# Splitting the last head's value product of an attention kernel into halves of two row tiles, with the turned weights' high half stored by key tile

## What is computed

```python
def _cross_attention(q_in, kv_in, wq, bq, wk, bk, wv, bv, wo, bo, bias_k, bias_v):
    ...
    logits = jnp.einsum('bqhk,bthk->bhqt', qh, kh) / scale
    weights = jax.nn.softmax(logits, axis=-1)
    ctx = jnp.einsum('bhqt,bthk->bqhk', weights, vh).reshape(b, q_len, H * K)
    return ctx @ wo + bo
...
    x = res + _cross_attention(h, xf_2, wq2, bq2, wk2, bk2, wv2, bv2, wo2, bo2, bias_k2, bias_v2)
    h = _layer_norm(x, ln_mlp_scale, ln_mlp_offset)
    h = jax.nn.gelu(h @ w_fc1 + b_fc1, approximate=False) @ w_fc2 + b_fc2
    return x + h
```

## Time and profile before

| | us |
|---|---|
| median of three runs (2645.69 to 2649.01) | 2648.83 |
| the profiled execution | 2647.3 |
| its span, from the first to the last instruction | 2645.5 |
| TensorE busy in it | 2588.6 |
| VectorE, ScalarE, GpSimd busy | 1724.0, 1506.7, 1321.5 |

### The profile page before, as it was taken

The page is one execution under the profiler, slowest core; times in us unless marked ns, Lnnn a source line. Parts: engine busy times, 40 slices in busy tenths (PEclk is TensorE's granted clock), DMA queues, the critical chain, the costliest instruction groups (busy, mean ns, idle before and its releaser), DMA issues.

```text
span 2645.5 us, 48709 instructions
## 1 busy us (share of the span) xinstructions
PE 2588.6 (98%) x17432; PEld 2144.1 (81%) x17432; DVE 1724.0 (65%) x2630; ACT 1506.7 (57%) x2350; POOL 1321.5 (50%) x750
## 2 busy tenths in 40 slices
PE   7999999999999999998999999999999999999989
PEld 6777788888888888886877777888888888888867
DVE  6999765656656656664279996665665665666641
ACT  4999555545445555544459994555545455555543
POOL 1244246666544666554613433466656456655634
PEclk9999999999999999999999999999999999999999
DMA  7312025345423445451462110344535134544411
GB/s 199 100 50 68 33 68 128 97 121 131 102 69 87 109 109 130 110 124 57 151 144 90 54 63 33 93 103 117 134 98 130 41 98 105 131 113 119 119 64 64
DMA packets 88386, 261.80 MB, mean 99 GB/s; under 512 B 20113, under 2 KB 33697, under 8 KB 81841
## 3 DMA queue, kind: packets, MB, share of 16 engines
q1 hardware_dynamic: 88240, 259.80, 36.9%
HBM read 135.45 MB, written 6.83 MB: 54 GB/s over the span
## 4 chain that ended last, share of the span: by engine, by line
PE 92%; DVE 3%; ACT 2%; issue 1%; DMA 1%; SPq 1%; POOL 1%; DVEq 0%; ACTq 0%; POOLq 0%
PE ps_m L1016 21%; PE ps_t L1016 19%; PE ps_s L1016 16%; PE ps_m L1260 7%; PE ps_t L1260 6%; PE ps_t L1140 6%; PE ps_m L1155 5%; PE ps_s L1124 4%; PE ps_m L1140 3%; PE ps_m L1193 1%; PE ps_m L1026 1%; POOL pT L503 1%; ACT pT L690 0%; ACT p L816 0%; DMA stg_qk<-in_w0q 0%
## 5 line engine op out<-in xcount | busy, mean ns | idle before, releaser
L503 POOL TENSOR_TENSOR pT<-pT,pT 128x1024 fp32r<-128x1024 f32 x224 | 540.1, 2411 | 505.3 <-ACT pT L690 500.7
L690 ACT ACTIVATE pT<-pT 128x1024 fp32r<-128x1024 f32 x224 | 237.9, 1062 | 319.6 <-DMA pT<-pb 319.6
L816 ACT ACTIVATE p<-ps_s,nm 128x1024 f32<-128x1024 f32 x256 | 284.8, 1113 | 201.0 <-DVE nm L1668 200.4
L1665 DVE TENSOR_REDUCE nmx<-ps_s 128x1 f32<-128x1024 f32 x256 | 309.8, 1210 | 119.9 <-PE ps_s L1016 119.8
L1016 PE MATMUL ps_s<-kT,qT 128*128 128x512 f32 x1536 | 384.2, 392 | 3.0 <-DVE qT L1650 3.0
L1684 DVE STREAM_TRANSPOSE pb<-p 128x1024 f32<-128x1024 f32 x224 | 278.1, 1241 | 104.7 <-ACT p L816 100.6
L1016 PEld LDWEIGHTS ps_s<-kT,qT 128*128 128x128 f32 x1536 | 281.5, 188 | 60.0 <-DVE qT L1650 4.7
L1592 DVE CUSTOM_DVE_ANT_0 sm<-ps_s,mask 128x1024 f32<-128x1024 f32 x256 | 309.7, 1210 | 5.7 <-PE ps_s L1124 3.0
L772 ACT ACTIVATE p<-sm,nm 128x1024 f32<-128x1024 f32 x256 | 293.7, 1147 | 33.1 <-DVE nm L1592 29.4
L1016 PE MATMUL ps_t<-ctxT,wa 128*128 128x512 f32 x1080 | 256.7, 391 | 0.0
L1016 PE MATMUL ps_m<-hT,wa 128*128 128x512 f32 x1008 | 243.1, 392 | 3.6 <-ACT g L978 3.6
(11 more groups left out here) (144 smaller groups left out, 4462.1 us busy)
## 6 DMA issues: line engine op xcount, KB each, us to landing
pT<-pb SPq DMA_DIRECT2D x896, 128.0 KB, 2.3
stg_qk<-in_wqk SPq DMA_DIRECT2D x40, 1024.0 KB, 7.5
stg_vo<-in_wo SPq DMA_DIRECT2D x48, 512.0 KB, 3.5
wob<-in_wo SPq DMA_DIRECT2D x32, 512.0 KB, 3.6
stg_vo<-in_wv SPq DMA_DIRECT2D x32, 512.0 KB, 3.6
q_stack<-scr_q SPq DMA_DIRECT2D x48, 128.0 KB, 4.0
st_ctx<-in_ctxT SPq DMA_DIRECT2D x8, 512.0 KB, 5.8
bv_row<-scr_bv SPq DMA_DIRECT2D x32, 128.0 KB, 5.7
```

What stands on the lines that cost most here:

```text
L503: return nc.gpsimd.tensor_tensor(out, x, f32(hi), ALU.subtract)
L690: return nc.scalar.activation(out, in_, ACT.Copy)
L816: nc.scalar.activation(p[t % 2][:], ps_s[t % 2][:], ACT.Exp, bias=nm[:, i:i + 1], scale=SCALE1, accum_out=sums[:, i:i + 1]).then_inc(exp_d ...
L1665: nc.vector.tensor_reduce(nmx[:, i:i + 1], ps_s[t % 2][:], AX.X, ALU.max, negate=True)\
```

## The change

The high half `pT[0]` is stored by key tile, `[P, ST, 4, P]`, so that what one matmul streams lies in one piece; the low half keeps its layout, because the DMAs write it. The value product now leaves its columns in the stored order, and `hi_c` and `lo_c` put them into the order of the rows when they read PSUM. In the tail before the MLP the last head's product is done in two halves of two row tiles (`values_half`, 256 columns), the first of them ahead of tile 3's turn. Each half goes by half-size copies into `qT[0]`, which is no longer needed there, and its two outputs follow it. Outputs 2 and 3 of the first head move between these steps. VectorE's statistics and aggregates of rows 0 and 1 are taken between the halves, and those of rows 2 and 3 after them, so `norm` has no aggregate left to make. After the root ScalarE runs a Gelu of one element per partition into a new tile `ahead`, whose result nobody reads.

```diff
--- before.py
+++ after.py
@@ -62,8 +62,8 @@
...
 L_K0, L_PV1, L_OUT1, L_K1, L_V, M_LAST = (15, 17), 16, (18, 19, 20, 21), (22, 23), (24, 25), 26
-E_V2, E_V3, E_PV0, E_T0, E_T1, E_OUT0, E_T2, E_T3 = 0, 1, 2, 3, 5, (7, 8, 9, 14), 10, 12
-E_PV1, E_OUT1, M_END = 15, (16, 17, 18, 19), 20
+E_V2, E_V3, E_PV0, E_T0, E_T1, E_OUT0, E_T2, E_T3 = 0, 1, 2, 3, 5, (7, 8, 14, 18), 9, 12
+E_PV1, E_OUT1, M_END = (11, 17), (15, 16, 19, 20), 21
 M_S = [M_START0, M_START0 + M_START - 2 + PAIRS * M_PAIR - M_PAIR + M_LAST]
@@ -122,6 +122,7 @@
...
         cols0q = sb("cols0q", [P, 4], F32)
+        ahead = sb("ahead", [P, 1], F32)
         ones = sb("ones", [P, P], F32)
@@ -181,7 +182,7 @@
...
         turned_at = at[0]
-        pT = sb("pT", [P, 4, ST * P], F32R, 2)
+        pT = [sb("pT_hi", [P, ST, 4, P], F32R), sb("pT_lo", [P, 4, ST * P], F32R)]
         pb = sb("pb", [P, 4, ST * P], F32)
@@ -248,7 +249,7 @@
...
         moved_hi, moved_lo = sem("moved_hi"), sem("moved_lo")
-        px_done, c_hi = sem("px_done"), sem("c_hi")
+        px_done, c_hi, c_half = sem("px_done"), sem("c_hi"), sem("c_half")
         bv_made, bv_out = sem("bv_made"), sem("bv_out")
@@ -305,7 +306,30 @@
...
-            return x[:].rearrange("p j (s t n) -> p s j t n", s=ST, t=LT)[:, 4 * q:4 * q + 4, :, lt, :]
+            if x == 0:
+                return pT[0][:].rearrange("p s j (t n) -> p s j t n", t=LT)[:, 4 * q:4 * q + 4, :, lt, :]
+            return pT[1][:].rearrange("p j (s t n) -> p s j t n", s=ST, t=LT)[:, 4 * q:4 * q + 4, :, lt, :]
+        def high_block(j):
+            return pT[0][:, :, j, :]
+        def low_block(j):
+            return pT[1][:, j, :].rearrange("p (s n) -> p s n", s=ST)
+        def in_rows(x):
+            return x.rearrange("p (j t n) -> p t j n", j=4, t=LT)
+        def of_rows(x):
+            return x[:].rearrange("p (t j n) -> p t j n", t=LT, j=4)
+        def half_in_rows(x):
+            return x[:, 0:256].rearrange("p (j t n) -> p t j n", j=4, t=2)
+        def half_of_rows(x, i):
+            return x[:, i * 256:(i + 1) * 256].rearrange("p (t j n) -> p t j n", t=2, j=4)
@@ -591,7 +615,7 @@
...
                             pool.wait_ge(moved_hi, 4 * x + j + 1)
-                            lo(pT[1][:, j, :], f32(pT[1][:, j, :]), pT[0][:, j, :]).then_inc(moved_lo, 1)
+                            lo(low_block(j), f32(low_block(j)), high_block(j)).then_inc(moved_lo, 1)
@@ -825,12 +849,12 @@
...
                             act.wait_ge(m_filled, rt + n + q + 1)
-                            copy(turned_in(pT[0], q, t % LT), turned_from(bank1(n + q))).then_inc(t_hi, 1)
+                            copy(turned_in(0, q, t % LT), turned_from(bank1(n + q))).then_inc(t_hi, 1)
...
                             act.wait_ge(moved_in[j], 64 * (x + 1) + 16)
-                            copy(pT[0][:, j, :], f32(pT[1][:, j, :])).then_inc(moved_hi, 1)
+                            copy(high_block(j), f32(low_block(j))).then_inc(moved_hi, 1)
@@ -840,7 +864,11 @@
...
                         act.wait_ge(m_filled, rt + n + 1)
-                        copy(cT[0][:], bank1(n)[:]).then_inc(c_hi, 1)
+                        copy(of_rows(cT[0]), in_rows(bank1(n)[:])).then_inc(c_hi, 1)
+                    def hi_c_half(n, i):
+                        act.wait_ge(m_filled, rt + n + 1)
+                        copy(half_of_rows(qT[0][0], i), half_in_rows(bank1(n))).then_inc(c_half, 1)
@@ -960,14 +988,19 @@
...
                     turned(n + (L_T2 if more else E_T2), 6)
+                    if not more:
+                        hi_c_half(n + E_PV1[0], 0)
                     turned(n + (L_T3 if more else E_T3), 7)
...
                         hi_column(n + L_K0[0], 1, 0, k_half(0, 0))
-                    hi_c(n + (L_PV1 if more else E_PV1))
-                    if more:
+                        hi_c(n + L_PV1)
                         hi_column(n + L_K0[1], 1, 0, k_half(0, 1))
+                    else:
+                        hi_c_half(n + E_PV1[1], 1)
+                        act.sem_inc(c_hi, 1)
                 root(b * ROWS + 3)
+                nc.scalar.activation(ahead[:], cols0q[:, 0:1], ACT.Gelu)
                 turn_hi(b * 3 + 2)
@@ -1249,7 +1282,7 @@
...
                         free1(n)
-                        out = bank1(n)[:].rearrange("p (t j n) -> p t j n", t=LT, j=4)
+                        moving = (lambda st: pT[0][:, st, :, :], lambda st: pT[1][:, :, st * P:(st + 1) * P])
                         for st in range(ST):
@@ -1257,18 +1290,29 @@
...
                             for i, (a, c) in enumerate(PASSES):
-                                mm = nc.tensor.matmul(out, v[a][:, st, h * P:(h + 1) * P],
-                                                      pT[c][:, :, st * P:(st + 1) * P]
-                                                      .rearrange("p j (t n) -> p t j n", t=LT),
+                                mm = nc.tensor.matmul(bank1(n)[:].rearrange("p (j n) -> p j n", j=4),
+                                                      v[a][:, st, h * P:(h + 1) * P], moving[c](st),
                                                       start=st == 0 and i == 0, stop=st == ST - 1 and i == 2)
...
-                    def output(ns, h, of, lts):
+                    def values_half(n, i):
+                        free1(n)
+                        for st in range(ST):
+                            moving = (pT[0][:, st, :, i * 64:(i + 1) * 64],
+                                      pT[1][:, :, st * P + i * 64:st * P + (i + 1) * 64])
+                            for k, (a, c) in enumerate(PASSES):
+                                mm = nc.tensor.matmul(bank1(n)[:, 0:256].rearrange("p (j n) -> p j n", j=4),
+                                                      v[a][:, st, P:2 * P], moving[c],
+                                                      start=st == 0 and k == 0, stop=st == ST - 1 and k == 2)
+                        mm.then_inc(m_filled, 1)
+                    def output(ns, h, of, lts, results=cT):
...
                             free1(n)
-                            passes(bank1(n)[:], lambda x, c: cT[x][:, lt * P:(lt + 1) * P],
+                            passes(bank1(n)[:], lambda x, c: results[x][:, lt * P:(lt + 1) * P],
                                    lambda q, c: wo[q][:, h, :], 1).then_inc(m_filled, 1)
@@ -1376,25 +1420,32 @@
...
                     pe.wait_ge(vo_lo, b * VO_B + 2 * f + 3)
-                    lts = LT if more else LT - 1
-                    output(out0[:lts], 0, n + (L_PV0 if more else E_PV0), range(lts))
-                    turned(n + (L_T2 if more else E_T2), 6)
-                    turned(n + (L_T3 if more else E_T3), 7)
                     if more:
+                        output(out0, 0, n + L_PV0, range(LT))
+                        turned(n + L_T2, 6)
+                        turned(n + L_T3, 7)
                         pe.wait_ge(qk_lo, 2 * (b * QK_B + 2 + f) + 4)
                         project_k(n + L_K0[0], 0, 0)
-                    else:
-                        output(out0[lts:], 0, n + E_PV0, range(lts, LT))
-                    freed(n + (L_T3 if more else E_T3) + 1)
-                    values(n + (L_PV1 if more else E_PV1), 1)
-                    if more:
+                        freed(n + L_T3 + 1)
+                        values(n + L_PV1, 1)
                         project_k(n + L_K0[1], 0, 1)
-                    output(out1, 1, n + (L_PV1 if more else E_PV1), range(LT))
-                    if more:
+                        output(out1, 1, n + L_PV1, range(LT))
                         for i in range(2):
...
                         project_v(n + L_V[0], 0)
+                    else:
+                        output(out0[0:2], 0, n + E_PV0, range(2))
+                        turned(n + E_T2, 6)
+                        freed(n + E_T1 + 1)
+                        values_half(n + E_PV1[0], 0)
+                        turned(n + E_T3, 7)
+                        for i in range(2):
+                            output(out0[2 + i:3 + i], 0, n + E_PV0, range(2 + i, 3 + i))
+                            output(out1[2 * i:2 * i + 2], 1, n + E_PV1[i], range(2 * i, 2 * i + 2), qT[0])
+                            if i == 0:
+                                freed(n + E_T3 + 1)
+                                values_half(n + E_PV1[1], 1)
@@ -1495,11 +1546,12 @@
...
-            def norm(k, eps):
-                for lt in range(LT):
+            def norm(k, eps, lts=range(LT)):
+                for lt in lts:
                     mm = nc.vector.bn_aggr(mean_var[:, lt, :], stats[:, lt, :])
-                link(mm)
+                if len(lts) > 0:
+                    link(mm)
                 nc.vector.tensor_scalar(lnv[:, 0, :], mean_var[:, :, 1], eps, 0.25, ALU.add, ALU.mult).then_inc(var_done, 1)
@@ -1671,8 +1723,8 @@
...
                             dve.wait_ge(t_hi, h0 + k + 2 * (t % LT) + q + 1)
```

(56 more changed lines are left out.)

## The result

The changed kernel takes 2630.69 us (median of four runs, 2628.61 to 2632.62), the kernel before 2648.06 beside it (2645.69 to 2649.01). The ratio is 0.9938, with a 95% interval of 0.9925 to 0.9950: 17.4 us less by the medians, 16.4 by the ratio. 2631 us had been forecast. The profiled execution took 2630.09 us, against 2647.3.

The account below looks back on a forecast made before the run. TensorE, busy 98% of the span, was taken to bound the loops, with hand-overs deciding outside them. Gains of 8.7 + 7.2 + 2.1 = 18.0 us from 2647.3 gave 2629.3, plus 1.5 for the median: 2631 us, range 2622 to 2641.

Parts of the forecast that it names:

- Part 1: Value products in the loops: high half stored by key tile, 5.46 us each instead of 5.60, gaining 8.7 us in all.
- rival (b): In the loops, GpSimd's subtraction slows on reading 8 runs and TensorE waits before first-head products: about 2684 us, 5%.
- TensorE has no idle time around them, so it all counts: In the loops, the whole 8.7 us saved on value products was claimed to shorten the kernel.
- the 0.3 named as a sign: In the loops, each turn 0.3 us shorter was to show that the value products had become faster.
- Rival (a): Value product: run count isn't what slows it, so the new layout gains nothing; 2639.5 us, 15%.
- Part 2: Tail, last head's product in halves: variance step 3.6 us sooner per batch, 7.2 us in all.
- the walk: Batch 0's tail followed hand-over by hand-over: halves start at 1210.8 and 1216.7, variance step at 1225.05 instead of 1228.70 us.
- The added wait: Tail: tile 3's copies queue behind the first half's, ready 1.9 us later, costing TensorE only 0.4 us.
- Rival (c): Tail: the halves bring nothing because copies queue on ScalarE and VectorE; 7.2 us lost, 2638 us, 6%.
- Part 3: MLP: one-element Gelu after the root loads the table ahead, saving 1.05 us per batch, 2.1 us in all.
- The clock at the turn: Before the MLP: first 16 hidden-projection matmuls take 6.11 or 3.91 us by clock, 2.2 us either way, outside the total.
- The sum: Whole kernel: 8.7 + 7.2 + 2.1 = 18.0 us saved, profiled execution 2629.3 us, median rounded to 2631.

Follow-up runs that it names:

- the two kernels with the early copy: Changed kernel with ScalarE's copy of the query weights' high half moved ahead of row tile 6's exponential, without and with 16 spare-bank matmuls before the turn: 2626.6 and 2620.42 us.
- early_filled: Changed kernel with ScalarE's query-weight high-half copy ahead of row tile 6's exponential, plus 16 matmuls into a spare bank before the turn: 2620.42 us, ratio 0.9897.

## Why the prediction came out, point by point

**Part 1: right cause, wrong size.** The product's length was forecast at 5.46 us and is 5.44 to 5.45. The reading of four runs costs nothing, where 1.2 ns had been taken. GpSimd's subtraction from 8 runs takes 2407 ns in the mean, as before (2411), so rival (b) has no ground, and the strided reads of PSUM were free as taken. The step that failed is "TensorE has no idle time around them, so it all counts". True of the kernel before, but a wait that was met by 0.04 us is as invisible as one that is met by 2. The cover of the value product's own inputs had been worked out (1.31 us), that of the projection behind it had not. The loops gave 6.2 us instead of 8.7, and a turn of the loop became 0.17 us shorter instead of the 0.3 named as a sign. Without the wait (early_filled) they gave 10.5: the 12 matmuls behind a product also became shorter there, 2.72 us instead of 2.76, beside the 0.15 of each product. The wait comes 24 times, six turns in each of the four loops, and costs 0.13 to 0.20 us of a turn, some 4 us; the two kernels with the early copy are 4.1 and 4.2 us below those without.

**Rival (a)** is refuted twice: by the result and by going back to 16 runs of 32, which cost 5.4 us. The Trainium skill's rule behind it ("SBUF — State Buffer", "Door 1: The DMA port swizzle"), full rate as long as consecutive accesses share a 16-byte line, does not account for this operand: a matmul takes 233.3 ns in runs of 32 and 226.7 in runs of 64 or more, though both are made of whole lines. From 64 elements on longer runs bring nothing more.

**Part 2: right.** The tail was to be 3.6 us shorter and is 3.75 and 3.77. The order of the walk holds: the first half starts 5.45 us behind the first turned block (forecast 5.5), tile 3 is ready at 10.98 (11.0), the second half starts at 11.37 (11.4). The added wait, put at 0.4 us of TensorE's time, costs it nothing: TensorE does not stand still between the start of the first half and the end of the second, since tile 3 is ready while it still makes outputs. Rival (c) is out.

**Part 3: right in its mechanism, short in its effect.** The wait fell from 1.8 to 0.8 us, 1.0 a batch. The Trainium skill ("ScalarE: Activation LUTs", "What ACT_TABLE_LOAD costs") adds a drain of about 1.38 us to every switch of tables, by which an estimate of this part would be 2.4 us a time. No such drain shows in the 1.0 us that came. What was not foreseen is the 1.5 us that come with it in batch 1, where the clock was low in the MLP and no longer is. The sum had no term for a clock fall after the gap.

**The clock at the turn** was said to be open either way by 2.2 us a batch. It went against the change in batch 1 (5.59 instead of 3.91 us) and slightly for it in batch 0. The gap before the turn was to be about 0.6 us shorter. The prediction's own walk gives 1.2 (last output filled at 1222.5, turn 1.86 us behind the variance step of 1225.05), and 1.24 came, 4.38 instead of 5.62. The shorter gap counts in the tail, but it gained nothing on the clock; only work in the gap did. Whether the clock is still low in the projection varied: with the gap of 4.38 us, the first 16 matmuls took 5.3 to 5.8 us (from the first start to the seventeenth) in 10 of 16 batches profiled, and 3.7 in the other six; with the gap of 5.6 us they took 5.8 to 5.9 in 2 of 8. That is too few to say whether the shorter gap made it likelier, so this loss may be chance or the change's own.

**The sum.** In the profiled executions 18.0 us were forecast, 17.2 came: 2.5 less in the loops, 0.3 more in the tail; Gelu's 2.0 as taken, less 1.3 lost to the clock at the turn, plus 1.5 in the MLP; and 1.2 in stages that nothing touched. So the exact hit on the median owes something to errors that cancel. (The chances of faster, same and slower, 92, 3 and 6%, add up to 101%.) What was right without luck is which parts count, their order of size, and the tail's walk.

## What to carry to other kernels

When a piece on the bounding engine gets shorter, look up every wait that stands right behind it, not only those in front: the cover to check is the time between the releaser's end and the first instruction that needs it, and a cover of a few hundredths is a wait to come. Where TensorE has to wait some microseconds for other engines, matmuls into a spare bank can be worth more than shortening the wait. And whether a strided operand costs anything is read from the distance between matmul starts, before a layout is rebuilt for it.

## What the runs showed of the hardware

- A matmul of 512 four-byte columns with new weights each time starts 226.7 ns after the one ahead (5.44 / 24) when its moving operand comes in 1 and 4 runs or in 8 runs of 64, 233.3 ns with 16 runs of 32, whether the high half's pieces lie together or apart and whether PSUM is written in one run or 16, and 231.7 ns with 32 runs of 16. In matmuls of 256 columns 8 runs of 32 cost nothing. Writing PSUM in 16 runs of 32 is free.
- ScalarE, VectorE and GpSimd read and wrote the same data in 4 to 8 runs, or in runs of 32 from PSUM, in the same time as in one.
- A gap of 4.38 us ahead of the turn left the clock at 1.2 GHz in most of the turn in all 16 batches profiled, and into the projection behind it in 10 of them. With matmuls in the gap until 0.70 to 0.76 us before the turn the clock was 2.4 GHz throughout in all four, for 3.0 to 3.1 us a batch against the changed kernel.
